# Storing the turned row maxima from ScalarE's DMA queue in place of SyncE's

## The reference

```python
x = x + tanh(g_xattn) * attention(layernorm(x), ctx, ctx, mask, Wq, Wk, Wv, Wo)
x = x + tanh(g_ffn) * ffn(layernorm(x), w_gate, w_up, w_down, ln_weight)
# attention: 16 query heads in 4 groups, head size 32
scores = q @ k.T / sqrt(32) + alibi_slope * (key - query), masked
w = softmax(scores); out = (w @ v) @ Wo
# ffn: every linear on int8-like rounded rows and ternary weights
h = silu(bit_linear(x, w_gate)) * bit_linear(x, w_up); out = bit_linear(rms_norm(h), w_down)
```

## Time and profile before

| what | us |
|---|---|
| median of 3 runs | 525.8 |
| lowest and highest of them | 525.53, 526.49 |
| the profiled execution | 528.64 |
| its span, first to last instruction | 526.5 |
| TensorE busy in the span | 472.9 (90%) |
| VectorE, ScalarE, GpSimd busy | 368.2, 320.2, 231.1 |

### The profile page before, as it was taken

How to read it: one execution, slowest core, us unless ns; L and a number is a source line. 1 busy time by engine, 2 the same in 40 slices (tenths; PEclk the granted TensorE clock), 3 DMA queues, 4 the chain that set the end, 5 groups by cost and what they waited for, 6 DMA issues and landing times.

```text
span 526.5 us, 8312 instructions
## 1 busy us (share of the span) xinstructions
PE 472.9 (90%) x2854; PEld 304.0 (58%) x2854; DVE 368.2 (70%) x674; ACT 320.2 (61%) x560; POOL 231.1 (44%) x250
## 2 busy tenths in 40 slices
PE   0799979998889898979899999888999999999966
PEld 0799979998875454545445545434454555555522
DVE  3887634464656698958788895387777777777762
ACT  1466627564545476646756766667777777777760
POOL 1000000000127777654536473147777677777630
PEclk9999999999798899989989999999999999999988
DMA  7889797999836969878768851012534333333223
GB/s 189 222 271 397 264 355 275 248 343 319 209 72 150 212 158 229 202 189 177 155 148 182 154 160 74 29 31 42 135 85 91 90 90 90 90 89 91 67 54 70
DMA packets 62833, 85.49 MB, mean 162 GB/s; under 512 B 37362, under 2 KB 48834, under 8 KB 61006
## 3 DMA queue, kind: packets, MB, share of 16 engines
q1 hardware_dynamic: 57614, 59.87, 45.7%
q0 software_dynamic: 3456, 12.58, 8.7%
q10 hardware_dynamic: 1728, 12.58, 6.8%
HBM read 57.94 MB, written 9.85 MB: 129 GB/s over the span
## 4 chain that ended last, share of the span: by engine, by line
PE 54%; DMA 14%; ACT 12%; DVE 12%; issue 5%; SPq 2%; POOL 0%; ACTq 0%; POOLq 0%; DVEq 0%
PE wide L1459 8%; DMA ct<-ctx_t 7%; PE bank L1381 6%; PE bank L1286 6%; PE bank L1369 6%; PE wide L1286 6%; PE wide L1355 5%; PE bank L1384 5%; PE bank L1327 5%; PE bank L1469 4%; DMA qs<-nm_t 4%; ACT p_t L724 3%; DMA wq_f<-wq 2%; DVE row_max L1020 1%; ACT sq_junk L846 1%
## 5 line engine op out<-in xcount | busy, mean ns | idle before, releaser
L1020 DVE TENSOR_REDUCE row_max<-wide 100x2 f32<-100x722 f32 x128 | 110.3, 902 | 29.5 <-PE wide L1355 28.9
L724 ACT ACTIVATE p_t<-bank 121x400 f32<-121x400 f32 x192 | 91.5, 506 | 59.4 <-PE bank L1369 56.6
L1459 PE MATMUL wide<-w_q,xq 128*128 128x512 bf16 x384 | 86.9, 380 | 2.7 <-DVE h L1137 2.4
L575 POOL TENSOR_TENSOR z<-h,lnw 128x512 f32<-128x512 f32 x48 | 61.1, 1275 | 15.1 <-DVE h L1137 14.5
L1459 PEld LDWEIGHTS wide<-w_q,xq 128*128 128x128 bf16 x384 | 35.5, 98 | 51.6 <-DVE h L1137 7.9
L1369 PE MATMUL bank<-qs,ks 103*121 103x400 f32 x144 | 53.0, 398 | 12.0 <-ACT p_t L724 5.7
L529 POOL DMA_DIRECT2D quant_in<-w_ffn x24 | 14.3, 597 | 102.1 <-PE bank L1327 95.6
L1327 PE MATMUL bank<-wv_f,ct 128*121 128x128 f32 x384 | 48.5, 287 | 3.7 <-DMA ct<-ctx_t 3.7
L1369 PEld LDWEIGHTS bank<-qs,ks 103*121 103x121 f32 x144 | 26.1, 189 | 44.3 <-issue 15.5
L1327 PEld LDWEIGHTS bank<-wv_f,ct 128*121 128x121 f32 x384 | 47.8, 198 | 4.3 <-DMA ct<-ctx_t 4.3
L967 DVE TENSOR_TENSOR ctl<-ct,cth 128x1445 fp32r<-128x1445 f32 x16 | 26.6, 1664 | 32.2 <-ACT cth L634 32.2
(11 more groups left out here) (160 smaller groups left out, 917.8 us busy)
## 6 DMA issues: line engine op xcount, KB each, us to landing
quant_in<-w_ffn POOLq DMA_DIRECT2D x24, 512.0 KB, 6.5
ct<-ctx_t SPq DMA_DIRECT2D x16, 722.0 KB, 10.8
abs_b<-w_ffn ACTq DMA_DIRECT2D x7, 1024.0 KB, 9.5
ks<-k_all SPq DMA_DIRECT2D x36, 181.0 KB
q_scratch<-qhl SPq DMA_DIRECT2D x16, 400.0 KB, 7.9
abs_a<-w_ffn ACTq DMA_DIRECT2D x5, 1024.0 KB, 8.0
qs<-q_scratch SPq DMA_DIRECT2D x12, 400.0 KB
xb<-x SPq DMA_DIRECT2D x12, 256.0 KB, 2.8
```

The lines of the kernel that those rows point to most:

```text
L575: nc.gpsimd.tensor_tensor(z[par][0:rows, c], h[0:rows, c], lnw[0:rows, c], ALU.mult).then_inc(z_done, 1)
L724: nc.scalar.activation(p_t[:, j, :], bank[j % 2][0:KT, 0:HQ], ACT.Exp).then_inc(exp_done, 1)
L1020: nc.vector.tensor_reduce(row_max[b % 2][:, 2 * u:2 * u + 2], wide[u % 2][0:SQ, :, 0:SK], AX_X, ALU.max).then_inc(s_maxed, 1)
L1459: mm = nc.tensor.matmul(wide[j % 2][0:rows, m, :], xq[par][:, c, 0:rows], w_q[:, m * C + c, 512 * j:512 * j + 512], start=(c == 0), stop=( ...
```

## The change

SyncE no longer stores the maxima of batches 2 to 15. In their place ScalarE, right behind its copy into `nm_t`, waits for that copy to be complete and issues the same two DMAs on its own queue, before its next exponential. The maxima of batches 0 and 1 stay with SyncE. What is stored, and who waits for it, is the same.

```diff
--- before.py
+++ after.py
@@ -426,8 +426,6 @@
                     store_max(0)
                     sp.wait_ge(kl_ready, B)
                     load_qk(LATE_SLOT)
-                elif b > 2:
-                    store_max(b - 1)
                 if 2 <= b < B - 2:
                     sp.wait_ge(st_done, (b - 1) * UNITS)
                     load_qk(b + 2)
@@ -728,6 +726,11 @@
                 if b > 0:
                     act.wait_ge(nm_in, b * 32)
                 copy_high(nm_t[:, :], turned_at(b)).then_inc(nm_ready, 1)
+                if b >= 2:
+                    act.wait_ge(nm_ready, b + 1)
+                    for part in range(2):
+                        act.dma_start(qs[b % SLOTS][ROWS_S + part:ROWS_S + part + 1, :, :].bitcast(F32).rearrange("p g (h q) -> p (g h) q", h=HPG),
+                                      nm_t[H * part:H * part + H, :].bitcast(F32)).then_inc(nm_in, 16)
 
             def keep_pv(b):
 
```

## The result

The changed kernel takes 537.88 us (median of 4 runs, 533.95 to 543.12), the kernel before beside it 526.14 us (4 runs). The ratio is 1.0245, with a 95% interval of 1.019 to 1.030: about 12 us slower, clear of the noise (that it is more than 2% this pair alone does not settle). Medians here are of all executions of a kernel; ratios and intervals compare only the faster ones, since some executions of either kernel take several us more. In a later group of runs the same pair gave 538.13 against 524.2, ratio 1.027 (1.0205 to 1.034). The profiled execution after took 537.52 us with a span of 535.7, against 528.64 and 526.5 before, so profile against profile it is 8.9 us; the profiled execution before was itself 2.5 us above its median. The forecast was 531.3, 5.5 us above the median before: right in sign, about half the size, with the result at the upper end of the range of 523.8 to 538.

A forecast was written before the change was run, and what follows sets the result against it. Bound by late maxima stores stalling TensorE and by tight ScalarE-TensorE pairing. -9.2 (store pauses, half clock) + 13.3 (ScalarE issues) = +4.1: 532.7 from the profile, 529.9 if the median lacks its surplus otherwise; middle 531.3 us, range 523.8 to 538.

The forecast's parts named there:

- the pauses of the store: TensorE's three waits at line 1369 for the stored maxima, 2.06, 1.25 and 2.42 us, would all go: 5.73 us.
- the half clock behind them: TensorE returning at 1.2 GHz after two of three store waits; its 3.45 us would be won too.
- the pause of ScalarE: Wait and two issues between copy and unit 6's exponential make unit 8 1.18 us later per plain step, 13.3 in all.
- The landing: The store on ScalarE's idle queue would land about 2.1 us after issue, in place of 6.7 behind load_qk.
- the slack of 0.14 us: Between unit 6's exponential ending on ScalarE and TensorE's unit 8 starting; anything ScalarE does before that exponential comes through.
- The price of an issue: One store issue on ScalarE costs 0.59 us, the median of SyncE's 24 issues of the same transfer.
- The other bound: One store issue on ScalarE costs only 0.335 us, as a large load there; the loss is then 7.2 us.
- The sum of the pauses: ScalarE's delay of unit 8: ten plain steps 11.8 us, batch 11 0.51, batch 14 1.02, batches 10 and 15 none; 13.3.
- the earlier trace: Kernel before's profile: a store landed after 2.1 us with q1 at 4.6% and q0 at 59.5%, read as own-queue backlog.
- the third rival: New TensorE pauses bring half clock; 1.68 us in half of ten steps adds 8.4, giving 539.7 us; chance 0.10.
- The second: Store shares engines with load_qk and lands as late as before: 13.3 - 3.5 = +9.8, 535.6 us; chance 0.10.
- The cheap issue: ScalarE issues at 0.335 us: loss 7.2 against gain 9.2, -2.0, giving 523.8 or 526.6 us; chance 0.17.

The follow-up runs named there:

- the spare transfer: Kernel before, SyncE still storing, with two ScalarE transfers of constants to unused scratch behind each copy of batches 2 to 15: 532.54 us, ratio 1.018.
- the repeat: The changed kernel run again without an edit in a later group: 538.13 us, ratio 1.027; its profiled execution took 546.75 us.
- dummy work: Changed kernel with two more ScalarE issues per batch (578.78 us), then with ten unread TensorE matmuls ahead of unit 8 added: 553.94 us, ratio 1.060.
- three complete kernels tried here: Kernel before with GpSimd's weight loads held for the store, load_qk's keys issued behind the store, or units 0 and 1 later: 526.97, 524.41, 524.32 us.

## Why the prediction was right in sign and wrong in size

Two steps failed, and they did not weigh the same. Term by term, for the stretch of the balance, the forecast had -5.7 for the pauses of the store, -3.45 for the half clock behind them and +13.3 for the pause of ScalarE, +4.1 in all; measured were -5.2, +3.6 and (as the remainder) +11.8, +10.2 in all, of which 1.3 us came back elsewhere (8.9 from profile to profile). The clock term is off by 7 us and alone makes the forecast too small. The landing was wrong as a mechanism but cost the sum only 0.5 us in this profile, which was luck: the very pause that the prediction charged as a cost hid most of the lateness.

- **What bounds the stage, and the slack of 0.14 us.** Right. In the plain steps what ScalarE does between copy and unit 6 came through.
- **The price of an issue, 0.59 us from SyncE's row.** Right: 0.606 and 0.568. The other bound, 0.335 from a large load, would have misled; the spare transfer, of another shape, took 0.39 on the same engine, and 0.58 behind the two of the store. So the price of this transfer is the same from either issuer, and that of another is not to be taken from it; what sets it stays open.
- **The sum of the pauses, 13.3 us.** The plain step grew by the 1.18 us forecast. The step behind the copy of batch 11 is 11.74 against 11.23 (0.51 forecast), that behind batch 14 is 11.75 against 10.74 (1.02 forecast). In all 11.8 by the balance above. The step of batch 9, which the prediction counted as plain, shows why it can be less: TensorE was at half clock there from 256 us on, and unit 8 did not wait.
- **"By the earlier trace rows it lands about 2.1 us after issue ... -9.2 us."** The landing failed. The store landed after 4.7 us on the own queue, and landings of 4 us and more were named as the sign that the relief is wrong. The earlier trace rows is a window whose total load was passing, and I read it as a window of one free queue. The DMA share right behind that issue was 0.17 and then 0.03, as shown with the weight loads above. Without the weight loads SyncE's queue gives 2.3 us and ScalarE's 2.5. The Trainium skill's page "DMA: Bandwidth & Descriptors", section "Issuing engines are not separate DMA queues", says that transfers of different issuers run on the same 16 DMA engines and interleave, and the traces agree with it: 4.7 us from ScalarE, 4.4 from SyncE with nearly the same pause. The pauses of 5.7 us did go in the first profile, but through the new pause; in the repeat 2.7 us of such pauses were left.
- **The clock behind a pause, the step that made the size wrong.** "All three pauses go, with the half clock behind two of them", and no term for half clock behind ten new pauses. The 3.45 us counted as won were not: missing clock rose by 3.6 in the first profile and by 12.6 in the second. In the first, half clock stands behind two of the eleven new waits, at 218 and 232 us; its two other stretches, at 256 and 273, stand behind waits of 2.05 and 1.00 us that the kernel before has as well. In the second it stands behind five waits of 0.91 to 0.93 us and one of 1.49. The forecast gave the clock no cost and the third rival 0.10. Its evidence, one pause of 1.25 us without a fall and one window at 1.00, was two draws of something that varies from run to run; the earlier trace rows already held one fall. The term should not have been nothing. As an estimate made with the result known: a third of ten new pauses at 1.68 us is 5.6 us, which with the sum makes 536.9.
- **The rivals.** The second (no relief, 535.6), as to the landing, and the third (half clock) happened together. The cheap issue is excluded by the measured 0.6 us an issue.

## What to carry to other kernels

On two engines that hand work to each other without slack, a DMA issue costs its full time in the issuing stream (0.6 us here) wherever the handed item stands behind it. The same two issues one instruction later cost 7 to 9 us less. A regular idle gap of a microsecond in TensorE's stream has to be priced with the clock: count what the gap may do to the matmuls behind it. The small transfer was late here because of the bytes under way on the shared engines, and another queue did not help. Moving those bytes does, but look which load then comes late: none of the three complete kernels tried here got faster by it.

## What was not expected of the hardware

The mean clock of the stage fell steeply with the length of a repeated pause: with about 0.3 us at unit 8 it was 0.97, as in the kernel before, with 0.92 it was 0.95 and 0.90 in two executions, with 2.06 it was 0.76. These are single profiles. Idle in front of unit 8 cost more than dummy work there: 578.8 us against 553.9. The changed kernel without the weight loads had 0.93, between the two of the full one, so the traffic is not seen to matter. What decides in which step the clock falls stays open: waits of the same 0.92 us had half clock behind them in some steps and not in others.
